# Layer 2's score matmuls, two heads at a time: two 32-row tiles and two banks in alternation, each bank also taking its head's transposed probabilities

## What is computed

```python
def _L2_gnn_ref(h, adj, Wq, bq, Wk, bk, Wv, bv, Wo, bo):
    NUM_HEADS, D_HEAD = 8, 32
    q = split_heads(h @ Wq.T + bq)
    k = split_heads(h @ Wk.T + bk)
    v = split_heads(h @ Wv.T + bv)
    scores = jnp.einsum('bhqd,bhkd->bhqk', q, k) * (1.0 / np.sqrt(D_HEAD))
    scores = jnp.where((adj == 0)[None, None, :, :], -jnp.inf, scores)
    attn = jax.nn.softmax(scores, axis=-1)
    out = jnp.einsum('bhqk,bhkd->bhqd', attn, v)
    out = out.transpose(0, 2, 1, 3).reshape(b, n, D_MODEL)
    return out @ Wo.T + bo
```

## Time and profile before

| | before |
|---|---|
| median of 3 runs | 1984.97 us |
| the profiled execution, its own time | 1986.96 us |
| its span | 1985.3 us |
| PE (TensorE matmuls) busy | 1872.7 us, 94% |
| DVE (VectorE) busy | 1727.5 us, 87% |
| ACT (ScalarE) busy | 1450.5 us, 73% |
| POOL (GpSimd) busy | 607.5 us, 31% |
| mean granted TensorE clock | 0.974 of full speed |
| moved by DMA | 43.85 MB, 22 GB/s |

### The profile page before, as it was taken

How to read it: one execution, slowest core, us unless ns; L and a number is a source line. 1 busy time by engine, 2 the same in 40 slices (tenths; PEclk the granted TensorE clock), 3 DMA queues, 4 the chain that set the end, 5 groups by cost and what they waited for, 6 DMA issues and landing times.

```text
span 1985.3 us, 45990 instructions
## 1 busy us (share of the span) xinstructions
PE 1872.7 (94%) x15944; PEld 1772.0 (89%) x15944; DVE 1727.5 (87%) x6095; ACT 1450.5 (73%) x3378; POOL 607.5 (31%) x756
## 2 busy tenths in 40 slices
PE   0789999999999999999999999999999999999965
PEld 0789999999999999999999999999999999998864
DVE  6678999999999999999999999999999989999743
ACT  2347787777777877787787777778877777787653
POOL 4112332323333223333332323333223333322222
PEclk8789999999999999999999999999999999999887
DMA  5000000000000000000000000000000000000000
GB/s 158 9 13 11 23 23 17 18 23 13 22 23 23 18 17 23 23 12 22 23 21 19 18 23 12 22 23 23 17 18 23 23 12 23 18 17 18 12 16 11
DMA packets 31206, 43.85 MB, mean 22 GB/s; under 512 B 3328, under 2 KB 26880, under 8 KB 30976
## 3 DMA queue, kind: packets, MB, share of 16 engines
q1 hardware_dynamic: 30976, 40.91, 6.4%
HBM read 32.38 MB, written 8.52 MB: 21 GB/s over the span
## 4 chain that ended last, share of the span: by engine, by line
PE 78%; DVE 8%; ACT 5%; issue 5%; POOL 1%; DMA 0%; DVEq 0%; ACTq 0%; POOLq 0%; SPq 0%
PE ps L900 54%; PE ps L929 13%; PE ps L1094 8%; PE ps L1113 3%; DVE lg L1367 2%; ACT pT L861 2%; ACT ea L808 1%; DVE tb L1296 1%; DVE cx L1387 1%; ACT pb L853 1%; ACT ea L799 0%; PE ps L1002 0%; DVE fu L1333 0%; DVE hT L1220 0%; DVE pT L1375 0%
## 5 line engine op out<-in xcount | busy, mean ns | idle before, releaser
L853 ACT ACTIVATE pb<-lg,hmin 128x256 f32<-128x256 f32 x512 | 232.1, 503 | 67.4 <-DVE hmin L1367 67.0
L1094 PE MATMUL ps<-kp,qp 32*128 32x256 f32 x1536 | 251.7, 296 | 3.3 <-DVE hmin L1367 1.7
L708 POOL TENSOR_SCALAR ea<-ea,rs 128x256 f32<-128x256 f32 x256 | 144.2, 575 | 356.7 <-DVE rs L1317 356.6
L735 POOL TENSOR_TENSOR fu<-fu,b_b 128x256 f32<-128x256 f32 x64 | 45.9, 738 | 674.1 <-PE ps L929 674.1
L861 ACT ACTIVATE pT<-ps 128x512 f16<-128x512 f32 x256 | 151.1, 590 | 133.3 <-PE ps L1113 67.4
L1367 DVE CUSTOM_DVE_ANT_0 lg<-ps,maskp 128x256 f32<-128x256 f32 x512 | 195.3, 419 | 55.6 <-PE ps L1094 55.6
L1094 PEld LDWEIGHTS ps<-kp,qp 32*128 32x128 f32 x1536 | 199.3, 186 | 39.4 <-issue 12.3
L900 PE MATMUL ps<-wout,hid 128*128 128x256 f32 x1536 | 219.7, 289 | 3.3 <-ACT hid L867 2.6
L900 PE MATMUL ps<-pT,whs 128*128 128x256 f32 x1536 | 212.6, 288 | 4.8 <-DVE pT L1326 3.0
L900 PE MATMUL ps<-wh,hT 128*128 128x256 f32 x1536 | 205.0, 286 | 0.4 <-DVE cols L1267 0.3
L692 POOL TENSOR_TENSOR rstd<-ve,pow_half 128x2 f32<-128x2 f32 x160 | 118.4, 741 | 280.4 <-DVE ve L1198 280.3
(11 more groups left out here) (180 smaller groups left out, 4683.3 us busy)
## 6 DMA issues: line engine op xcount, KB each, us to landing
tbc<-t_dram SPq DMA_DIRECT2D x32, 512.0 KB, 3.6
xin<-x_in SPq DMA_DIRECT2D x32, 256.0 KB, 2.8
out<-xs SPq DMA_DIRECT2D x32, 256.0 KB, 2.2
t_dram<-tb SPq DMA_DIRECT2D x128, 1.0 KB
xs<-a_heads SPq DMA_DIRECT2D x4, 128.0 KB, 6.3
pT<-a_heads SPq DMA_DIRECT2D x4, 128.0 KB, 5.0
lg<-W_out SPq DMA_DIRECT2D x2, 256.0 KB, 5.5
tb<-adj SPq DMA_DIRECT2D x1, 256.0 KB, 2.8
```

The lines of the kernel that those rows point to most:

```text
L708: last = pool.tensor_scalar(ea(g)[:, c, :], ea(g)[:, c, :], rs[g][:, c:c + 1], 1.0, ALU.mult, ALU.mult)
L853: last = act.activation(pb[h % 2][:, c, :], lg[h % 2][:, c, :], ACT.Exp, bias=hmin[h % 2][:, c:c + 1], scale=-1.0)
L1094: last = pe.matmul(bank(BA)[:, c, :], qp[r, a, oc, blk(c)], kp[r, b, oc, :], start=(n == 0), stop=(n == 2))
```

## The change

The scores of heads 2p and 2p + 1 become one step. Its 12 matmuls alternate between the two heads: one matmul of head 2p, whose operands lie in one 32-partition group and whose output goes to bank BA, then one of head 2p + 1, in the next 32-partition group and bank BB. Each head's transposed probabilities now go to the bank that held its own scores. So the transposes of a head no longer wait for the head before it (its bank was read by its own `smin`), while a pair's scores wait for `pT16_lo` of the second head of the pair before. `smin`, `pT16_hi` and `pT16_lo` read the bank of their head. In the planner a pair's scores are entered at 0.8 us, where one head's had 0.7, with the new waits, and the four LEADs are other numbers.

```diff
             for h in range(HQ):
-                a("scores", h, TE, 0.7, ("q_lo", 0), ("k_lo", 0), ("smin", h - 1))
-                a("smin", h, VE, 0.69, ("scores", h), ("s_exp", h - 2))
+                if h % 2 == 0:
+                    a("scores", h // 2, TE, 0.8, ("q_lo", 0), ("k_lo", 0), ("pT16_lo", h - 1))
+                a("smin", h, VE, 0.69, ("scores", h // 2), ("s_exp", h - 2))
                 a("s_exp", h, SC, 0.8, ("smin", h), ("p_T", h - 2))
-                a("p_T", h, TE, 0.44, ("s_exp", h), ("pT16_lo", h - 1))
+                a("p_T", h, TE, 0.44, ("s_exp", h))
...
-        GRAIN, LEAD = 0.02, (42.0, 28.0, -2.0, 23.0)
+        GRAIN, LEAD = 0.02, (47.0, 41.0, 32.0, 30.0)
...
+        def head_bank(h):
+            return BB if h % 2 else BA
...
-                    act.activation(pT16[h % 2][:, 0], bank(BB), ACT.Copy).then_inc(pT16_hi, 1)
+                    act.activation(pT16[h % 2][:, 0], bank(head_bank(h)), ACT.Copy).then_inc(pT16_hi, 1)
...
-                def scores(h, u):
-                    if h == 0:
+                def scores(p, u):
+                    if p == 0:
                         pe.wait_ge(q_lo, u + 1)
                         pe.wait_ge(k_lo, u + 1)
                     else:
-                        pe.wait_ge(min_ready, of(u, h - 1, HQ))
-                    r, oc = slice(DH * (h % 4), DH * (h % 4) + DH), h // 4
+                        pe.wait_ge(pT16_lo, of(u, 2 * p - 1, HQ))
                     for c in range(C):
                         for n, (a, b) in enumerate(PARTS):
-                            last = pe.matmul(bank(BA)[:, c, :], qp[r, a, oc, blk(c)], kp[r, b, oc, :],
-                                             start=(n == 0), stop=(n == 2))
+                            for h in (2 * p, 2 * p + 1):
+                                r, oc = slice(DH * (h % 4), DH * (h % 4) + DH), h // 4
+                                last = pe.matmul(bank(head_bank(h))[:, c, :], qp[r, a, oc, blk(c)], kp[r, b, oc, :],
+                                                 start=(n == 0), stop=(n == 2))
                     last.then_inc(s_done, 1)
 
                 def transpose_probs(h, u):
                     pe.wait_ge(p_done, of(u, h, HQ))
-                    if h:
-                        pe.wait_ge(pT16_lo, of(u, h - 1, HQ))
-                    transpose_to(BB, pb[h % 2]).then_inc(p_turned, 1)
+                    transpose_to(head_bank(h), pb[h % 2]).then_inc(p_turned, 1)
...
                 def score_minimum(h, u):
-                    dve.wait_ge(s_done, of(u, h, HQ))
+                    dve.wait_ge(s_done, of(u, h // 2, HQ // 2))
...
-                            out=lg[h % 2][:, c, :], in0=bank(BA)[:, c, :], in1=maskp[:, c, :],
+                            out=lg[h % 2][:, c, :], in0=bank(head_bank(h))[:, c, :], in1=maskp[:, c, :],
...
-                    dve.tensor_tensor(pT16[h % 2][:, 1], bank(BB), pT16[h % 2][:, 0], ALU.subtract)\
+                    dve.tensor_tensor(pT16[h % 2][:, 1], bank(head_bank(h)), pT16[h % 2][:, 0], ALU.subtract)\
```

## The result

The changed kernel takes **1952.0 us** in the median of its runs (1949.99 to 1954.13) against 1985.0 for the kernel before: a ratio of 0.983 with an interval of 0.981 to 0.984. It is faster by 33 us where 93 were forecast, and 1952 lies above the range.

A forecast was written before the change was run, and what follows sets the result against it. PE was taken as the bound, 56.7 us of work in 57.34 a graph. Period falling from 57.27 to 54.6 over 31 intervals (83 us) plus 10 at the start gave 93 us off: 1892 us, range 1864 to 1946.

The forecast's parts named there:

- PE's work: PE per graph: 56.7 us of work in a 57.34 us period falls by 3.9 to 52.8 us.
- the overlap with it: Scores steps: the two heads' tiles run beside each other, 12 matmuls in 0.81 us, a pair 1.17 instead of 2.14.
- Rival A: Scores matmuls stand in line, loads one by one or tiles not overlapping: period 56.3, 1945 us; chance 0.19.
- the reading of the load's price as 12 loads one by one: Scores weight loads: estimated 107 ns each, 1.28 us for a pair in place of 0.81 if they went singly.
- Rival C: Scores: every change of tile costs like a 128-to-32-row change, 0.18 us on each of 12 matmuls; 2177 us; chance 0.06.
- The price of a change between 128 and 32 rows: PE at each scores step: going from 128-row to 32-row work and back costs 0.36 us.
- The new wait: Pair's scores wait for the second head's low part before: chain 6.3 us, covered by PE's 7.9, 1.6 to spare.
- The ends: Start and tail: first graph's layer 3 starts 10 us earlier; the last layer 3 stays at 63.3 us.
- What is late next: DVE, nearly as full as PE: loss from mutual waiting grows from 0.6 to 1.8 us a graph, period 54.6 us.
- Nothing of that goes away: DVE's 52.6 busy us a graph: none is removed, since minima, low parts and gathers are the same instructions.
- the prediction's own sign: Profile after: 12 score matmuls taking 1.0 us while the period stays above 56 would mean DVE and the heads' chain bind.
- B: DVE and the heads' chain bind although tiles overlap: 3.4 us lost a graph, period 56.2, 1942 us; chance 0.15.

The follow-up runs named there:

- experiment 1: Changed kernel with the old four LEAD numbers: 2064.6 us; kernel before, single heads, with the new LEAD numbers: 2099.2 us.
- the new order: Changed kernel with the same instructions, its engine lists replanned from measured step durations with newly searched LEADs, second answer of the search: 1914.7 us.
- experiments 1 to 4: Against the kernel before: LEADs swapped 1.039, 1.056; pair's heads in line 1.0034; less DVE work 0.980, 0.993 (before), with less ACT 0.972; less PE work 0.975, 0.983 (before).
- experiment 7: 128x2 DVE product made two one-column instructions with per-partition scalar: on the changed kernel 1947.9 us, on its first replanned order 1904.4 us; two other grown DVE steps listed.

## Why the prediction was wrong

**PE's work: right, and the overlap with it.** A pair was to cost 0.81 + 0.36 = 1.17 us. It costs 0.92 in the chain, with the 0.17 in its neighbours 1.09. That makes 4 x 1.05 = 4.2 us a graph instead of 3.9, and 52.5 us of work instead of 52.8. Rival A fell (12 matmuls would take 1.6), and with it the reading of the load's price as 12 loads one by one, 1.28 us a pair, which was the estimate from the Trainium skill, "TensorE: Matmul & The Clock Gate", section "LDWEIGHTS (loading the stationary operand)". What the 0.19 us for two loads agrees with is Part 3 of the same page of the Trainium skill, on row groups side by side. Rival C fell wholly: no change of tile costs anything. The price of a change between 128 and 32 rows, 0.36, stayed about as it was (0.92 + 0.17 - 0.71 = 0.38).

**The new wait: right.** The scores steps wait 8.7 us in all for the low part of the pair before, over the whole program. The heads' steps themselves wait less than they did (beside the earlier trace rows; from the page's groups: busy us, mean ns, idle before):

```profile
L857 ACT ACTIVATE pb<-lg,hmin 128x256 f32<-128x256 f32 x512 | 222.2, 499 | 17.6 <-DVE hmin L1370 17.4
...
L1370 DVE CUSTOM_DVE_ANT_0 lg<-ps,maskp 128x256 f32<-128x256 f32 x512 | 188.7, 419 | 15.2 <-PE ps L1099 12.2
...
L1378 DVE TENSOR_TENSOR pT<-ps,pT 128x512 f16<-128x512 f32 x256 | 174.1, 682 | 11.2 <-ACT pT L865 11.0
```

**The ends: a term too small.** I took 10 us for the earlier first layer 3, from PE's work that no longer lies ahead of it; it was 18.9. The new numbers without the pairs give 15.8 of these (experiment 1), so less work on PE is not the only way to them. The tail was to stay and grew by 1.5, at a granted clock of 0.74 where it had been 0.79.

**The step that failed** is "What is late next": "Today 0.6 us is lost with a margin of 4 us on DVE; I take 1.8." Lost were 56.67 - 52.5 = 4.2 us a graph. 2.4 us times 31 are 74, which is more than the whole miss of 60; the better PE term (9) and the better start (9) gave some back, and the tail and the step from spans to medians take some 4 again. By rows 4 and their like after, PE stands idle for 2.5 us of a graph where it was 0.2; the other 1.7 lies inside its busy time, which counts each matmul to its modelled end, and was not taken apart. Two things were wrong in it.

- *The loss was sized from whole graphs.* Over a graph DVE had 2 to 4 us of room. But each engine runs a fixed list, and in the 23 us from 989.9 the list gives DVE 22.5 us of work and PE only 21.3. Where such stretches lie is decided by the order, and a graph costs at least what the busiest engine of each stretch asks, added up. That the order is the limit, and not the sum of any engine's work, is shown by the new order (same work, 37 us less) and experiments 1 to 4 fit it: 54 us less of DVE gave 5, 59 less of PE gave 15, and in the first of these the chain shows ACT in DVE's place.
- *"Nothing of that goes away" was taken to mean that DVE's time stays.* It grew from 52.6 to 54.2 us a graph. Over the whole program it is 46 us: 20 of them are the one step that POOL now holds up, 16 the two others of experiment 7, and the last 10 were not taken apart.

**The rivals.** A came nearest in time, 1945 us, with a mechanism that the runs refute. By the prediction's own sign, 12 matmuls at 1.0 us or less and a period above 56, it is B, 1942 us at 3.4 us lost, and B is half the mechanism: DVE is first in the 23 us stretch, but ACT follows at once, and the other 34 us are still PE's. I gave B 0.15. The range ended at the price of A, 1946 with rounding, because B was priced by a single guess of the loss, 3.4 us, and not by a bound. The trace of one order shows little of what another order loses, so that term deserved the widest bounds of the sum, not the narrowest.

What stays open: how the 4.2 us lost split between DVE, ACT and the hand-overs between them, and the pairing's worth between best orders.

## What to carry to other kernels

Where every engine runs a fixed list, ask of a saving on the full engine in which stretches the lists give the others as much to do: a saving there can be worth a part of itself (here a quarter to a half for layer 3's products), while a step that the others wait for can be worth all of it (here the scores). When a step's price changes, work the order out again and run old and new orders before you put a gain down to the step; a new search can also give a slower order, as it did for the heads. Look at the granted clock of each run too: one wait of 2.6 us a graph brought the lower level with it. Then look for DVE operations that start beside a long POOL operation, small ones with two SBUF tensors first, and after each edit check by line where the hold went.

## What the runs showed of the hardware

- Two 32-row tiles overlap by half even when their matmuls are issued one head after the other: twelve take 1.25 us, six take 0.90, and the second six begin about 0.35 us after the first.
- A DVE product of 128x2 numbers went from 0.16 to 0.92 us beside a POOL subtraction of 128x512, and to 1.25 in another order; as two products of 128x1, each with one SBUF tensor and a scalar operand per partition, it takes twice 0.21 and is not held (202 to 215 ns in 64 cases). A DVE `tensor_scalar` of 128x256 with one SBUF tensor can be held all the same: 0.41 us in the median, up to 1.48 beside POOL.
- Behind a pause of PE of 2.59 us the granted clock was 0.50 for 6.8 us, in a kernel whose clock was 1.00 for the rest of that graph.
